# Routed experts' weights streamed from DRAM as the stationary side, in a two-layer transformer kernel on one core

## The reference, cut to what matters

```python
def _swiglu(t, a, b, c):
    return jax.nn.silu(t @ a) * (t @ c) @ b
logits = xt @ gate_w.T
scores = jax.nn.softmax(logits, axis=-1)
topk_w, topk_i = jax.lax.top_k(scores, K)                 # K = 2 of E = 8
comb = jnp.zeros((T, E), x.dtype).at[jnp.arange(T)[:, None], topk_i].add(topk_w)
for e in range(E):
    y = y + comb[:, e:e + 1] * _swiglu(xt, w1[e], w2[e], w3[e])   # hidden size 352
return y.reshape(B, S, D) + _swiglu(x, sw1, sw2, sw3)             # hidden size 192
```

## Time and profile before

| | |
|---|---|
| median of three runs | 1226.88 us (1226.86 to 1234.54) |
| the profiled execution | 1231.06 us, its span 1229.0 us |
| TensorE busy | 1089.1 us, 89% of the span, 7912 records |
| its weight loads | 504.0 us, 41% |
| VectorE busy | 879.4 us, 72% |
| ScalarE busy | 775.3 us, 63% |
| GpSimd busy | 408.9 us, 33% |
| granted TensorE clock, mean | 0.933 |
| DMA | 119.36 MB, 59.26 MB read from DRAM |

### The profile page before, as it was taken

The page is one execution under the profiler, slowest core; times in us unless marked ns, Lnnn a source line. Parts: engine busy times, 40 slices in busy tenths (PEclk is TensorE's granted clock), DMA queues, the critical chain, the costliest instruction groups (busy, mean ns, idle before and its releaser), DMA issues.

```text
span 1229.0 us, 22171 instructions
## 1 busy us (share of the span) xinstructions
PE 1089.1 (89%) x7912; PEld 504.0 (41%) x7912; DVE 879.4 (72%) x1813; ACT 775.3 (63%) x1327; POOL 408.9 (33%) x462
## 2 busy tenths in 40 slices
PE   5588798889999898999989998989998999999985
PEld 3122222123444343444544545545554444544453
DVE  5899788878887676786657776667565777777354
ACT  3058577567766666568765665646766576776853
POOL 2000204250205326314246242351115652433352
PEclk8579898889999898999998999989998899999998
DMA  4705472533316125116144162451512615431110
GB/s 115 167 31 139 175 188 73 138 107 110 101 58 176 50 87 126 62 63 149 60 124 98 36 169 68 112 124 39 132 52 80 149 56 124 113 84 39 55 37 17
DMA packets 120699, 119.36 MB, mean 97 GB/s; under 512 B 17856, under 2 KB 102592, under 8 KB 120208
## 3 DMA queue, kind: packets, MB, share of 16 engines
q1 hardware_dynamic: 115280, 106.68, 32.7%
q0 software_dynamic: 4736, 10.49, 3.0%
q10 hardware_dynamic: 576, 0.79, 0.2%
HBM read 59.26 MB, written 58.62 MB: 96 GB/s over the span
## 4 chain that ended last, share of the span: by engine, by line
PE 47%; DMA 15%; DVE 13%; issue 9%; ACT 8%; POOL 5%; SPq 1%; POOLq 0%; ACTq 0%; DVEq 0%
PE ps L685 9%; PE ps L752 6%; DMA gr<-d_y,pos 6%; DVE nm L875 6%; PE ps L647 5%; PE ps L668 5%; PE ps L769 3%; ACT ES L1226 3%; PE ps L784 3%; DMA d_h<-hx,pos 3%; PE ps L777 2%; ACT xn L1161 2%; PE ps L713 2%; PE ps L759 2%; DMA d_u<-US 2%
## 5 line engine op out<-in xcount | busy, mean ns | idle before, releaser
L875 DVE TENSOR_REDUCE nm<-ps 128x2 f32<-128x1024 f32 (+3 forms) x512 | 508.7, 1018 | 110.9 <-PE ps L653 58.2
L1226 ACT ACTIVATE ES<-ps 128x1024 f32<-128x1024 f32 (+3 forms) x512 | 432.4, 864 | 172.5 <-PE ps L668 94.0
L685 PE MATMUL ps<-ES,VS 128*9 128x512 f32 (+3 forms) x2048 | 237.2, 539 | 1.1 <-DVE nmp L886 0.5
L647 PE MATMUL ps<-KS,QS 48*128 48x512 bf16 (+3 forms) x1024 | 185.6, 369 | 46.8 <-DVE nm L875 26.0
L668 PE MATMUL ps<-QS,KS 51*128 51x512 bf16 (+3 forms) x1024 | 179.9, 355 | 15.1 <-DVE nm L875 5.7
L752 PE MATMUL ps<-f,hsT 128*128 x368 | 142.5, 491 | 5.8 <-DVE nm L875 3.3
L647 PEld LDWEIGHTS ps<-KS,QS 48*128 48x128 bf16 x1024 | 50.5, 95 | 193.6 <-issue 64.3
L668 PEld LDWEIGHTS ps<-QS,KS 51*128 51x128 bf16 x1024 | 49.9, 95 | 177.7 <-issue 73.3
L1434 POOL TENSOR_TENSOR ya<-ya,yS 128x512 f32<-128x512 f32 x49 | 62.2, 1269 | 155.1 <-DVE yS L1121 154.9
L1355 POOL TENSOR_TENSOR sp<-sr,sp 128x512 bf16<-128x512 f32 x32 | 37.1, 1158 | 199.8 <-ACT sp L1202 199.5
L1391 POOL DMA_INDIRECT d_h<-hx,pos x64 | 63.2, 988 | 89.4 <-DMA d_h<-hx,pos 52.1
(11 more groups left out here) (190 smaller groups left out, 1471.7 us busy)
## 6 DMA issues: line engine op xcount, KB each, us to landing
d_u<-US SPq DMA_DIRECT2D x64, 256.0 KB
KS<-d_k SPq DMA_DIRECT2D x64, 192.0 KB
QS<-d_q SPq DMA_DIRECT2D x64, 192.0 KB
d_q<-sp SPq DMA_DIRECT2D x16, 384.0 KB
d_k<-sp SPq DMA_DIRECT2D x16, 384.0 KB
hs<-d_h SPq DMA_DIRECT2D x20, 256.0 KB
d_y<-ys SPq DMA_DIRECT2D x20, 256.0 KB, 2.3
d_q<-sp SPq DMA_DIRECT2D x16, 256.0 KB
```

Source lines behind the costliest of these rows:

```text
L647: mm = eng.matmul(psum[:, bank[u][a], 0:n], QS[m][r:r + KA, pr, 128 * t:128 * t + 128], KS[m][r:r + KA, pr, 0:n], start=True, stop=i < NB)
L685: mm = eng.matmul(psum[32 * a:32 * a + 9, b, q0:S], VS[i % 3][:, j, 4 * g + a, :], ES[(2 * (NT * (NG * i + g) + j) + a // 2) % NES][:, a % ...
L875: eng.tensor_reduce(nm[f][:, :].rearrange("p (a c) -> p a c", a=2)[:, :, 4 * pr + t], ps2("score", i, f, pr, t)[:, :, 0:n], AX.X, ALU.max, ...
L1226: eng.activation(ES[(2 * n + pp) % NES][:, :, 0:S - q0], ps2("bscore", i, f, g, j, pp)[:, :, 0:S - q0], ACT.Exp, scale=SC1 if i >= NB else ...
```

## The change

- The routed experts' weights no longer stay in SBUF. They lie in DRAM as `we`, 8 blocks of 128 x 1152 (gate, up and down, each 384 wide, padded from 352). A new step `x_w` on SP loads one tile's block (128 rows of 4608 bytes) into one of four buffers `wst` (`NST = 4`), after `x_dn` of the tile four back. The block's row is in a register of SP; `x_reg` is on SP and reads 12 registers.
- `x_up` has the weights as the stationary side: for each of gate and up, three matmuls of 128 x 128 against the tile's turned rows (128 moving columns). The result has the hidden features on the partitions, so `x_ht` and `x_hc` are gone and `x_dn` takes `hdx` as it is. `x_th`, `x_gate`, `x_mul` are 384 wide.
- `x_gate` waits for `x_dn` two tiles back where it waited for `x_ht`.
- The shared expert's weights are one tensor `fs`; the loads `f1`, `f3`, `f2`, `f1s`, `f3s`, `f2s` are gone.
- `NES` is 8, `expo` waits for `pv` of group n - 4. There are two buffers `hs`, eight `gr` (a gather waits for `g_w` four tiles back), and `hP` and `lat` have their own memory, so that `p_norm` no longer waits for the projections before it.
- The last image's borrowed buffers lie in `wst`; what waited for the last `x_up` or `x_dn` for them waits for the last `x_dn` that uses the buffer.
- The due times `SHIFT`, `LATE`, `LAST` and the second value of `SPREAD` are others; `LAST["x"]` and such entries apply by a step's second index.

```diff
-NES = 6
+NES = 8
+
+NST = 4
-SHIFT = {"t": -0.39, "s": 1.02, "p": -0.35, "stack": -0.35, "pv": 0.11, "f": 0.37, "d": 1.41, "x": 1.14, "max": -0.38, "r": 0.28, "rr": 0.28, "u": -0.15, "g": -0.54, "bscore": -0.08, "expo": -0.08}
-LATE = {"d": -0.05, "f": -0.22, "score": 0.12, "rowmax": 0.12, "t": 0.43, "max": 0.24, "g": 0.09, "u": 0.82}
-LAST = {"max": -0.08, "r": -0.06, "rr": -0.06, "pv": 0.15}
+SHIFT = {"t": -0.16, "s": 1.02, "p": -0.35, "stack": -0.35, "pv": 0.16, "f": 0.56, "d": 1.41, "x": 1.14, "max": -0.56, "r": 0.28, "rr": 0.28, "u": -0.15, "g": -0.57, "bscore": -0.08, "expo": -0.08}
+LATE = {"d": -0.05, "f": -0.22, "score": 0.1, "rowmax": 0.1, "t": 0.43, "max": 0.24, "g": 0.09, "u": 0.82, "s": -0.1}
+LAST = {"max": -0.08, "r": -0.06, "rr": -0.06, "pv": 0.15, "x": 0.14, "p": 0.05, "stack": 0.05, "d": 0.53, "s": -0.54, "t": -0.05, "u": -0.07}
...
-SPREAD = 2.4, 1.8
+SPREAD = 2.4, 2.3
...
-        add("ACT", ("p_norm", i), 0.9, i - 0.1, [("p_rstd", i), ("p_turn", i - 1)] + [("p_v", i - 1), ("p_proj", i - 1, 0), ("p_proj", i - 1, 1)])
+        add("ACT", ("p_norm", i), 0.9, i - 0.1, [("p_rstd", i), ("p_turn", i - 1)])
...
-                m = NT * (NG * i + g) + j - 3
+                m = NT * (NG * i + g) + j - NES // 2
...
-                        add("PE", ("x_reg", q, h), 2.0, u, [("rr_tex", q), ("x_dn", q - (h == 0), NMT - 1 if h == 0 else 11)])
+                        add("SP", ("x_reg", q, h), 1.0, u - 0.35, [("rr_tex", q), ("x_w", q - (h == 0), NMT - 1 if h == 0 else 11)], lag=0.1)
...
+                    n = NMT * q + j - NST
+                    add("SP", ("x_w", q, j), 0.5, u - 0.3, [("x_reg", q, h), ("x_dn", n // NMT, n % NMT)], lag=3.6)
...
-                        add("PE", ("x_up", q, j, c), 0.59, u, [("x_hst", q, L), ("x_reg", q, h), ("ld", f"f{2 * c + 1}"), ("x_gate",) + j2, ("x_ht",) + j2]
+                        add("PE", ("x_up", q, j, c), 0.68, u, [("x_hst", q, L), ("x_w", q, j), ("x_dn",) + j2]
...
-                    add("PE", ("x_ht", q, j), 0.34, u, [("x_mul", q, j), ("x_dn",) + j2], opens=1)
-                    add("ACT", ("x_hc", q, j), 0.37, u, [("x_ht", q, j), ("x_dn",) + j2], closes=[("x_ht", q, j)])
...
-                    v = eng.snap(rows[j % 12], min_val=0, max_val=7 * 352)
-                    eng.matmul(ps(*u)[:, 0:352], T_[:, a0:a0 + 128], (f1, f3)[c][:, bass.ds(v, 352)],
-                               start=True, stop=True).then_inc(s["x_up"], 1)
+                    for n in range(3):
+                        mm = eng.matmul(ps(*u)[:, 128 * n:128 * n + 128], wst[(NMT * p + j) % NST][:, c, 128 * n:128 * n + 128],
+                                        T_[:, a0:a0 + 128], start=True, stop=True)
+                    mm.then_inc(s["x_up"], 1)
...
+                    for n in range(3):
+                        mm = eng.matmul(ps(*u)[:, 0:128], hdx[(NMT * p + j) % 2][:, 128 * n:128 * n + 128],
+                                        wst[(NMT * p + j) % NST][:, 2, 128 * n:128 * n + 128], start=(n == 0), stop=(n == 2))
...
+                elif k == "x_w":
+                    p, j = u[1:]
+                    if NMT * p + j >= NST:
+                        q.wait_ge(*on("x_dn", *tile_before(p, j, NST)))
+                    v = eng.snap(tiles[j % 12], min_val=0, max_val=7 * 128)
+                    eng.dma_start(wst[(NMT * p + j) % NST][:, :, :].rearrange("p a b -> p (a b)"),
+                                  we[bass.ds(v, 128), :]).then_inc(slot(*u), 16)
```

More of the change, by code:

```diff
@@ L80, in add @@
             urgency += LAST.get(family, 0.0)
-        self.work[key] = (engine, weight, urgency, after, lag, mode, opens, closes)
+        self.work[key] = (engine, weight, round(urgency, 3), after, lag, mode, opens, closes)
     @staticmethod
@@ L164, in after_t, with last_in @@
     return ("t_rv" if T_ON_DVE[i] else "t_res", i)
+def last_in(m):
+    n = max(n for n in range(NB // 2 * NMT) if n % NST == m)
+    return n // NMT, n % NMT
 def plan():
@@ L188, in plan @@
     add("POOL", ("c_more", 1), 5.0, 0.5, [("c_more", 0), ("p_lo", 1, 1)])
-    load("f1", 2.0, 8.0, after=[("score", 2, 0, 0, 0)])
-    load("f3", 2.3, 8.0, after=[("score", 2, 0, 3, 0)])
-    load("f2", 2.6, 8.0, after=[("score", 2, 1, 0, 0)])
     for c in range(2):
@@ L419, in program @@
         w1s = sb("w1s", [128, W1N])
-        f1 = sb("f1", [128, 8 * 352 + 192])
-        f3 = sb("f3", [128, 8 * 352 + 192])
-        f2 = sb("f2", [128, E * 3 + 2, 128])
+        fs = sb("fs", [128, 640])
+        wst = [sb(f"wst{i}", [128, 3, 384]) for i in range(NST)]
         r1 = sb("r1", [128, E, 128])
@@ L456, in program @@
         hx = [sb(f"hx{i}", [128, NT, D]) for i in range(2)]
-        hs = sb("hs", [128, 4, D])
+        hs = [sb(f"hs{i}", [128, 4, D]) for i in range(2)]
         ys = [sb(f"ys{i}", [128, 4, D]) for i in range(2)]
@@ L460, in program @@
         cv = sb("cv", [128, NT, D])
-        gr = [sb(f"gr{i}", [128, D]) for i in range(4)]
+        gr = [sb(f"gr{i}", [128, D]) for i in range(8)]
         ohs = sb("ohs", [128, 2, 8, E])
@@ L465, in program @@
         pos = [sb(f"pos{i}", [128, 2, 8], U32) for i in range(2)]
-        tex = [sb(f"tex{i}", [128, 2, 24], U32) for i in range(2)]
+        tex = [sb(f"tex{i}", [128, 24], U32) for i in range(2)]
         rt = sb("rt", [128, 5, 64])
@@ L485, in program @@
         hd = [sb(f"hd{i}", [128, S]) for i in range(2)]
-        tx = [sb(f"tx{i}", [128, 352]) for i in range(2)]
-        hdx = [sb(f"hdx{i}", [128, 352]) for i in range(2)]
-        hxT = [sb(f"hxT{i}", [128, 384]) for i in range(2)]
+        tx = [sb(f"tx{i}", [128, 384]) for i in range(2)]
+        hdx = [sb(f"hdx{i}", [128, 384]) for i in range(2)]
         yT = sb("yT", [128, NT, 128])
@@ L542, in program @@
         rstd_a = {u: 2 * n + 1 for n, u in enumerate(u for u in todo["POOL"] if u[0] in ("p_rstd", "f_rstd"))}
-        for n in range(4):
+        for n in range(8):
             s["g_ga", n] = ctx.enter_context(nc.semaphore(f"g_ga{n}"))
@@ L579, in _ @@
             q = Queue(eng)
-            rows, cols = ([eng.alloc_register(f"row{k}_{n}") for n in range(12)] for k in range(2))
-            f2v = f2[:, :, :].rearrange("p a b -> p (a b)")
             def open_banks(u):
@@ L1033, in _ @@
                     if p >= 2:
-                        for n in range(4):
-                            q.wait_ge(s["g_ga", n], 16 * NT * (p - 1))
+                        for n in range(8):
+                            q.wait_ge(s["g_ga", n], 16 * 2 * (p - 1))
                     eng.tensor_copy(pos[p % 2][:, :, :], rt[:, 1, 0:16].rearrange("p (k t) -> p k t", k=2)).then_inc(s[k], 1)
@@ L1151, in _ @@
                         q.wait_ge(*on(("p_turn", "f_turn")[w], i - 1))
-                    if w == 0 and i:
-                        q.wait_ge(*on("p_v", i - 1))
-                        for n in range(2):
-                            q.wait_ge(*on("p_proj", i - 1, n))
                     if w == 1 and 0 < i <= NB:
@@ L1189, in _ @@
                     i = u[1]
-                    q.wait_ge(*on("p_turn", i))
                     q.wait_ge(*on("p_lat", i))
+                    if i > NB:
+                        q.wait_ge(*on("p_v", i - 1))
+                        for n in range(2):
+                            q.wait_ge(*on("p_proj", i - 1, n))
                     eng.activation(lat, ps("p_lat", i), ACT.Copy).then_inc(s[k], 1)
@@ L1454, in _ @@
             q = Queue(eng)
-            R0 = E * 352
-            loads = {"w0": (w0s[:, :], w0), "w1": (w1s[:, :], w1), "f1": (f1[:, 0:R0], wf1[:, 0:R0]), "f3": (f3[:, 0:R0], wf3[:, 0:R0]),
-                     "f2": (f2[:, 0:3 * E, :], wf2[:, 0:3 * E, :]), "f1s": (f1[:, R0:], wf1[:, R0:]),
-                     "f3s": (f3[:, R0:], wf3[:, R0:]), "f2s": (f2[:, 3 * E:, :], wf2[:, 3 * E:, :]), "r1": (r1[:, :, :], wr1), "r2": (r2[:, :, :], wr2),
+            tiles = [eng.alloc_register(f"tile{n}") for n in range(12)]
+            loads = {"w0": (w0s[:, :], w0), "w1": (w1s[:, :], w1), "fs": (fs[:, :], ws), "r1": (r1[:, :, :], wr1), "r2": (r2[:, :, :], wr2),
                      "bo": (bos[:, :, :], bo.partition_broadcast(128)), "c0": (cs[:, 0, 2, :], cT[0]), "c1": (cs[:, 1, 2, :], cT[1])}
```

170 lines of the change are left out of this document (73 added, 97 removed).

## The result

| | before | after |
|---|---|---|
| median | 1230.54 us (20 runs, 1223.08 to 1234.54) | 1236.69 us (20 runs, 1231.74 to 1242.15) |
| ratio after / before | | 1.0065, 95% interval 1.0046 to 1.0084 |
| span of the profiled execution | 1229.0 us | 1239.2 us |
| TensorE busy | 1089.1 us, 89% | 1067.6 us, 86% |
| TensorE idle (span less busy) | 139.9 us | 171.6 us |

The account below looks back on a forecast made before the run. TensorE, 93.5% busy in the tiles' stretch (290:935 us), was taken as the bound; -33 TensorE, -3 order and +6 traffic make -30 us, 1229.0 to 1199 profiled, forecast 1197 us from median 1226.9; 8-in-10 range 1172 to 1234.

Parts of the forecast that it names:

- Record costs: Up projections on TensorE: 4 float32 records per tile become 12, 1.19 us becomes 1.35, +15 us in all (upper end +28).
- the gaps at the register loads: TensorE's queue: eight pairs of register loads leave it; idle gaps near five total 10.1 us; taken as -8 us.
- That TensorE's time shows, -33: TensorE in the tiles' stretch: +15 up projections, -40 transposes, -8 register loads; ends -2 and -39 us.
- Buffers, 0 us: Eight exponential buffers, no wait shown for value products: 0 us directly; eight gather buffers: 0, with an end of -5.
- Order, -3 with +-10: Changed order on every engine from buffers and due times: -3 us, bounded by a third of 32 us idle time.
- Traffic, +6 with ends 0 and +23: 54 MB of tile weights on the shared DMA engines delay small chained transfers 0.25 us each: +6 us.
- a quarter shows: Of 23 us added latency on small transfers in the tiles' stretch, most lies beside other images' matmuls; a quarter counted, +6 us.
- B: TensorE's time falls, but DMA traffic and other engines' chains give back most: 1215 to 1234, middle 1222; chance 0.20.
- C: Slower: tile weights come late through SP's in-order queue, TensorE stands 2.6 us at one tile in four: 1257; chance 0.11.
- E: Up projections' 12 weight loads per tile into TensorE's array are not hidden, +90 us: 1309; chance 0.02.
- a busy share below 90% in the stretch: Sign against the forecast: TensorE's busy share in the tiles' stretch, 290:935 us, falling from 93.5% to below 90%.

Follow-up runs that it names:

- the stationary side: Kernel before with weights resident, up projections' weights as stationary side, no transposes or copies: 1228.01 us with old due-time tables, 1223.51 us with the changed kernel's.
- small loads: Changed kernel, same order, but from the fifth tile on each weight load brings 64 KB in place of 576 KB (stale weights): 1197.54 us, ratio 0.9742.

## Why the prediction was wrong, point by point

**Record costs: right.** +15 was said for the up projections, +16.6 of busy time was measured; twelve records that stand together take 1.50 to 1.60 us from first start to last end, a spacing of 0.11 to 0.12 us (less the last record's 0.28, over 11). The four records of before take 1.35 to 1.45 in the same view. The first lines of such pieces in the timeline of after:

```profile
307.21 1.60 PE L748 MATMUL ps<-hsT,wst 128*128 128x128 f32 x12
...
333.56 1.50 PE L748 MATMUL ps<-hsT,wst 128*128 128x128 f32 x12
```

The prediction's 1.35 us for such a piece was 12 spacings and left out that the last record lasts 0.28 us itself; for the difference to before that changes little, as the busy time shows. Transposes, copies and the gaps at the register loads are gone, as said; the 8 us put on the gaps weren't measured alone.

**That TensorE's time shows, -33: wrong in size.** The step "93.5% busy, and the work taken away stands in its queue" took nearly all of the saved work for saved time. What shows depends on the order. With the old tables the stationary side took 24 us of busy time away and 1.4 us of time (1228.01 against 1229.39), with the new ones 15.1 and 12.6. At the changed kernel's order three transposes a tile are worth 20.2 us, not 40. A busy share of 93.5% was read as a bound; with 42 us idle in the stretch, spread over waits for row maxima, exponentials and others, it was a near tie.

**Buffers, 0 us: wrong.** Eight exponential buffers, with the order that goes with them, are worth 14.6 us. The reason given, that ScalarE shows no wait for the value products, didn't bound it. That the planner had kept the exponentials behind the value products in the order itself, where no wait shows it, is likely but only argued. The other buffers, with the register loads off TensorE's queue, are worth about 1223.51 - 1212.14 = 11 us, from the stationary side with new tables to the streaming kernel with small loads and six such buffers; here too the order is another, and nothing separates the two.

**Order, -3 with +-10: wrong size.** It is worth 32 us here (1268.78 to 1236.69). The bound, a third of the stretch's idle time, assumed that an order can only use idle time that is there; a worse order makes new idle time.

**Traffic, +6 with ends 0 and +23: the step that failed, and that decided.** It cost 39.2 us, beyond its own upper end, and the 33 us between the two are nearly the whole distance from the forecast's -30 to the measured +6. Two factors failed. A hop's delay was put at 0.25 us; measured are 0.3 to 0.6 at medians and 2.2 at the results' stores. Only the hops of images were counted, not the 16 scatters and 16 gathers of a pair nor the stores ahead of the gathers. And "a quarter shows" had no row behind it. No term held the 10.5 us of busy time that TensorE gains with the traffic, at a clock in the stretch of 0.95 in place of 0.97. The load itself landed after 4.7 us (read where its median is given, in the kernel without landings on VectorE), near the 4.6 from the rows. The 3.4 us estimated from the Trainium skill (DMA: Bandwidth & Descriptors, Anatomy of one DMA) was too low; that section's figure is for transfers that GpSimd issues, and these are SP's. Without the traffic the kernel takes 1197.5 us, but that it meets the forecast's 1197 is luck: the parts without traffic summed to -36, and the measured -32 is -6 for stationary side and tables together, -11 for buffers and register loads, and -15 for the exponential buffers, each with its new order.

**The rivals.** B, that traffic and chains give the gain back, is what happened, with the size wrong: 1215 to 1234 was its range and 1236.7 the time, just outside the whole range too. Its sign was the one to read: its chance of 0.20 was too low, and its price was capped by a sum of few hops. C is refuted: loads land in 4.7 us, and all that any trace here lists of TensorE waiting for tile weights is 1.9 us before matmuls and 2.8 before weight loads with three buffers, and 0.4 before a weight load with the old tables. E is refuted by the spacing of 0.11 to 0.12 us under weight loads of 0.192. Of the signs named as proof against the forecast one came: a busy share below 90% in the stretch, 570.8/645 = 88.5%.

**What stays open:** through which chains the 39 us go. Not SP's ring (nothing gained from ScalarE's), not VectorE's queue alone (0 of 39), hardly the gathers (some 4, by the intervals up to 7); the scatters, the results' stores (2.2 us later each) and the lower clock are left, and it may be many hops together.

## What to carry to other kernels

Streaming weights that used to be resident isn't free merely because the DMA engines are at 60% and the loads arrive in time: price the bytes by what they do to every other transfer that stands in a chain, and test it by shrinking the loads at a fixed order, which costs one kernel. An engine at 93% busy is not by that alone a bound whose work can be taken off one for one: here it was worth 1 of 24 us at one order and 13 of 15 at another. Waits that rise in step with the time aren't their cause until a kernel without them has been run at both ends.

## What was not expected of the hardware

- With four indirect transfers of GpSimd under way and small loads, ScalarE and VectorE stand up to 5.2 us at waits for TensorE whose matmuls had ended, and TensorE behind them up to 7.7 us; in one stretch of 20 us during the scatters (705 to 725) its granted clock was 0.50 to 0.53, the lower of its two levels, after a slice with 7.0 us busy in 10. Waits of this kind come to 0 to 15 us in the kernels with two under way. What holds them up isn't known.
- In the two kernels without landings on VectorE the tile loads of 576 KB land in 4.7 us and those of 64 KB in 2.5, and the stores of 256 KB beside them in 4.7 and 2.5 us, while stack loads of 192 KB hardly differ.
- The price of background bytes sets in early: 16.4 us for the first 23 MB (88 loads, 256 KB more each), 22.8 for the next 23, and for the copy of 54 MB 65.4, or 28 for each 23. Whether it rises or is even can't be told, with intervals of 5 to 7 us.
